# A two-level search for the first edges of quads, slot tables built group by group, degrees counted in a later pass

## The reference

```python
edge_index = jnp.stack([src, dst])
x = layernorm(x + L0(x, edge_index, edge_attr))
x = layernorm(x + L1(x, edge_index))
# L0: e = edge_attr @ W_edge + b_edge; msg = relu(x[src] + e)
#     agg = segment_sum(msg, dst); h = (1 + eps) * x + agg
#     h = relu(h @ W1 + b1) @ W2 + b2; batch norm over nodes, relu
# L1: deg = segment_sum(1, dst) + 1; dinv = rsqrt(deg)
#     layer(h, W, b): h = h @ W.T
#       agg = segment_sum(h[src] * dinv[src] * dinv[dst]) + own row; relu(agg + b)
#     three such layers
```

## Time and profile before

| | us |
|---|---|
| median of 3 runs | 4261.39 (4259.22 to 4263.67) |
| the profiled execution, its own time | 4236.74 |
| its span, first to last instruction | 4235.0 |
| PE, DVE, ACT, POOL busy, share of the span | 89%, 88%, 63%, 51% |
| constants | 0 to 21 |
| degrees | 21 to 196 |
| slot tables | 196 to 268 |
| GIN pass | 268 to 1475 |
| batch norm's scale | 1475 to 1488 |
| norm pass | 1488 to 2036 |
| three GCN passes | 2036 to the end |

### The profile page before, as it was taken

The page is one execution under the profiler, slowest core; times in us unless marked ns, Lnnn a source line. Parts: engine busy times, 40 slices in busy tenths (PEclk is TensorE's granted clock), DMA queues, the critical chain, the costliest instruction groups (busy, mean ns, idle before and its releaser), DMA issues. The chain is left out here.

```text
span 4235.0 us, 107970 instructions
## 1 busy us (share of the span) xinstructions
PE 3771.7 (89%) x27934; PEld 3481.4 (82%) x27934; DVE 3713.5 (88%) x10654; ACT 2649.3 (63%) x6276; POOL 2170.3 (51%) x1972
## 2 busy tenths in 40 slices
PE   6639999999999889999688889869889988999999
PEld 1139999999999768888688888868888887888887
DVE  8838898889889799999788888868888887999999
ACT  0016666666666578888677878757878885444444
POOL 0035444444444000000477777757777775777776
PEclk9869999999999989999899999989999999999999
DMA  0055555555555299999677767747767776999999
GB/s 24 1 98 166 162 159 158 158 158 159 160 159 159 70 324 375 374 374 376 217 211 214 214 211 218 213 151 213 217 208 215 219 216 197 315 311 309 312 311 287
DMA packets 871189, 909.87 MB, mean 215 GB/s; under 512 B 154170, under 2 KB 770580, under 8 KB 871060
## 3 DMA queue, kind: packets, MB, share of 16 engines
q1 hardware_dynamic: 744400, 702.74, 50.8%
q0 software_dynamic: 94080, 205.13, 17.9%
q10 hardware_dynamic: 32580, 0.52, 0.5%
HBM read 651.69 MB, written 308.28 MB: 227 GB/s over the span
## 5 line engine op out<-in xcount | busy, mean ns | idle before, releaser
L462 POOL DMA_INDIRECT rows<-ga_scratch,node_i x980 | 1081.4, 1103 | 997.5 <-POOLq L598 699.6
L462 POOL DMA_INDIRECT rows<-x_in,node_i x490 | 518.5, 1058 | 671.6 <-DVE raw L915 476.8
L462 POOL DMA_INDIRECT rows<-gb_scratch,node_i x490 | 567.1, 1157 | 182.3 <-issue 171.9
L490 PE MATMUL gcn_agg_ps<-gcn_rows_hi,gcn_select 128*128 128x256 f32 x2156 | 576.5, 302 | 33.9 <-DVE gcn_rows_lo L1260 33.9
L490 PE MATMUL gcn_agg_ps<-gcn_rows_lo,gcn_select 128*128 128x256 f32 x2156 | 542.8, 286 | 0.0
L1380 PE MATMUL fin_agg_ps<-rows,fin_select 128*128 128x256 f32 x2156 | 530.8, 380 | 0.0
L1279 ACT CAST gcn_rows_hi<-rows 128x768 fp32r<-128x768 f32 (+1 forms) x392 | 286.2, 731 | 331.9 <-DMA rows<-ga_scratch,node_i 162.3
L1380 PEld LDWEIGHTS fin_agg_ps<-rows,fin_select 128*128 128x128 f32 x2156 | 410.8, 191 | 56.2
L490 PEld LDWEIGHTS gcn_agg_ps<-gcn_rows_hi,gcn_select 128*128 128x128 f32 x2156 | 419.4, 195 | 34.8 <-DVE gcn_rows_lo L1260 34.8
L517 PE MATMUL gcn_g_ps<-g_hi,gcn_ht_hi 128*128 128x256 f32 x1568 | 441.7, 282 | 0.7 <-ACT gcn_g L1298 0.7
L862 ACT ACTIVATE h1t_hi<-h1t_ps,b_sb 128x256 fp32r<-128x256 f32 x392 | 164.8, 471 | 439.0 <-issue 346.2
(11 more groups left out here) (158 smaller groups left out, 12314.2 us busy)
## 6 DMA issues: line engine op xcount, KB each, us to landing
own<-x_in SPq DMA_DIRECT2D x196, 256.0 KB, 3.0
h_scratch<-h2t SPq DMA_DIRECT2D x196, 256.0 KB, 2.2
h2t_in<-h_scratch SPq DMA_DIRECT2D x196, 256.0 KB, 3.9
x_sb<-x_in SPq DMA_DIRECT2D x196, 256.0 KB, 4.9
x_scratch<-x SPq DMA_DIRECT2D x196, 256.0 KB, 5.0
ga_scratch<-g_out SPq DMA_DIRECT2D x196, 256.0 KB, 5.1
gcn_own<-ga_scratch SPq DMA_DIRECT2D x196, 256.0 KB, 2.9
gb_scratch<-gcn_g SPq DMA_DIRECT2D x196, 256.0 KB
```

Of the source, the lines that this page charges most:

```text
L462: pool.indirect_dma_start(out=c["rows"][:, slot, b], out_offset=None, in_=source[:, :], in_offset=bass.IndirectOffsetOnAxis(ap=c["node"][: ...
L490: last = nc.tensor.matmul(out[:, j], select[:, b, j * P:(j + 1) * P], rows[:, pair.odd + b], start=n == 0, stop=n == len(terms) - 1)
```

## The change

- `degrees` and `slot_tables` go; `search` takes their place. It loads only the destinations (a new input array `dst`), as 128 rows of 392. For each of the 98 quads, and each of the five tile limits 0, 128, ..., 512 from the quad's first node, a one-hot matrix chooses the row in which the limit lies, five float32 products on PE fetch these rows, and DVE counts the entries below the limit. First edges and the test for `fast` come from that.
- In the GIN pass the windows are loaded four quads at a time: SP loads group 0 ahead of the pass and group g + 2 at the beginning of group g, ACT loads group 1 ahead of its first step. DVE makes the tables of group g + 1 (seven operations on 20 columns) at the beginning of group g, ahead of the step's h0; at group 0 it makes those of group 0 as well. POOL waits for them once a group.
- The degrees are counted in the norm pass. DVE splits `place` into tile and node once; POOL writes five one-hot matrices of 128 columns for a quad; PE adds five products with 4 columns for a quad at the head of the even steps; DVE copies the counts, ACT takes the root and DVE does the Newton step for 16 tiles once a group.
- `general_sum` counts a histogram of its own in its first use, under `fast == 0`, and is skipped as before.

```diff
-def pipeline(eng, step):
+def pipeline(eng, step, begin=None):
     def group(number):
+        if begin is not None:
+            begin(number)
         for k in range(GROUP):
...
-def degrees(nc, keep, dram):
+def search(nc, keep, dram):
...
+                sp.dma_start(dst_i[:, 0:COLS], dram["dst"][0:P * COLS].rearrange("(p c) -> p c", p=P))
+                sp.dma_start(dst_i[:, COLS:COLS + 2],
+                             dram["dst"][COLS:COLS + P * COLS].rearrange("(p c) -> p c", p=P)[:, 0:2])
...
+                nc.vector.tensor_copy(rows[:, 0:COLS + 1], dst_i[:, 0:COLS + 1])
+                nc.vector.tensor_scalar(upto[:], limit[:], rows[:, COLS:COLS + 1], None, ALU.is_le)
+                nc.vector.scalar_tensor_tensor(out=chosen[:], in0=limit[:], scalar=rows[:, 0:1], in1=upto[:],
+                                               op0=ALU.is_gt, op1=ALU.mult)
+                nc.vector.tensor_tensor(falls[:], rows[:, 0:COLS], rows[:, 1:COLS + 1], ALU.is_gt)
+                nc.vector.tensor_reduce(broken[:, 6:7], falls[:], AX.X, ALU.add)
+                nc.vector.tensor_tensor(less[0:NQ], found[0:NQ, :, 0:COLS], own_limit..., ALU.is_lt)
+                nc.vector.tensor_reduce(count[0:NQ], less[0:NQ], AX.X, ALU.add)
+                nc.vector.tensor_tensor(partly[0:NQ], count[0:NQ], found[0:NQ, :, COLS + 2], ALU.mult)
+                nc.vector.tensor_tensor(before[0:NQ], partly[0:NQ], found[0:NQ, :, COLS + 1], ALU.add)
+                nc.vector.tensor_scalar(rel[0:NQ], before[0:NQ, 1:TILES + 1], before[0:NQ, 0:1], None, ALU.subtract)
...
+                for t in range(TILES + 1):
+                    nc.tensor.matmul(found[0:NQ, t, 0:COLS + 3], chosen[:, t:t + NT]..., rows[:])
+                nc.tensor.matmul(start_row[0:1, 0:NQ], before[0:NQ, 0:1], c["ident"][0:NQ, 0:NQ])
+                nc.tensor.matmul(broken_sum[:], c["ones"][:], nbroken[:])
...
# gather_quads
+        if tables is not None and quad % GROUP_QUADS == 0:
+            pool.wait_ge(tables, (quad // GROUP_QUADS + 1) * TABLE_STEPS)
...
# gin_pass, SP
+                def begin(number):
+                    if not isinstance(number, int) or number + 2 < TABLE_GROUPS:
+                        sp.wait_ge(windows_in, (number + 1) * LANDED)
+                        load_windows(sp, number + 2, windows_in)
+                load_windows(sp, 0, windows_in)
+                pipeline(sp, step, begin)
...
# gin_pass, ACT
+                load_windows(act, 1, windows_next)
...
# gin_pass, DVE
+                def begin(number):
+                    if isinstance(number, int) and number == 0:
+                        table(0)
+                    if not isinstance(number, int) or number + 1 < TABLE_GROUPS:
+                        table(number + 1)
...
# norm_pass, POOL
+                pool.wait_ge(split_done, 5)
+                for quad in range(NQ):
+                    if quad >= 2:
+                        pool.wait_ge(counted, quad - 1)
+                    for b in range(BLOCKS):
+                        last = nc.gpsimd.tensor_scalar(hot_node[:, quad % 2, b], c["iota16"][:, 0:P],
+                                                       node_in_tile[:, quad, b:b + 1], None, ALU.is_equal)
+                    last.then_inc(hot_done, 1)
...
# norm_pass, ACT
+                    if (pair := at(8)) and pair.place == 0:
+                        act.wait_ge(deg_steps, pair.group * DEG_STEPS + 1)
+                        nc.scalar.activation(root[:], deg[:], ACT.Sqrt).then_inc(rooted, 1)
...
# norm_pass, PE, first in the step
+                    if (pair := at(0)) and not pair.odd:
+                        pe.wait_ge(hot_done, pair.quad + 1)
...
+                        for b in range(BLOCKS):
+                            last = nc.tensor.matmul(deg_ps[:, first:first + 4], hot_node[:, pair.quad_slot % 2, b],
+                                                    hot_tile[:, bass.ds(pair.quad, 1), b]...)
+                        last.then_inc(counted, 1)
...
# norm_pass, DVE: seven operations on 490 and 1960 columns ahead of the steps (place to node_in_tile, hot_tile)
+                    if (pair := at(7)) and pair.place == 0:
+                        dve.wait_ge(counted, (pair.group + 1) * GROUP_QUADS if whole else NQ)
+                        nc.vector.tensor_tensor(deg[:], deg_ps[:, 0:GROUP_TILES], c["hist"]..., ALU.add)
+                    if (pair := at(9)) and pair.place == 0:
+                        degree(pair)   # reciprocal, mult, add, scale, reciprocal on 16 columns, each behind a wait
...
# gnn
-        degrees(nc, keep, dram)
-        slot_tables(nc, keep, dram)
+        search(nc, keep, dram)
```

More of the change, by code:

```diff
@@ L320, in _ @@
+                nc.vector.tensor_tensor(falls[:], rows[:, 0:COLS], rows[:, 1:COLS + 1], ALU.is_gt).then_inc(chain, 1)
                 dve.wait_ge(chain, 6)
[L321 to L329 removed]
@@ L453, in gather_quads @@
-def gather_quads(nc, pool, c, source, gathered, rows_free):
+                pe.wait_ge(chain, 5)
+                for t in range(TILES + 1):
+                    nc.tensor.matmul(found[0:NQ, t, 0:COLS + 3],
+                                     chosen[:, t:t + NT].rearrange("p (q t) -> p q t", t=TILES)[:, :, 0],
+                                     rows[:], start=True, stop=True).then_inc(looked, 1)
+                pe.wait_ge(chain, 11)
+                nc.tensor.matmul(start_row[0:1, 0:NQ], before[0:NQ, 0:1], c["ident"][0:NQ, 0:NQ],
+                                 start=True, stop=True).then_inc(looked, 1)
@@ L455, in gather_quads @@
+                pe.wait_ge(chain, 14)
+                nc.tensor.matmul(broken_sum[:], c["ones"][:], nbroken[:], start=True, stop=True).then_inc(looked, 1)
+def gather_quads(nc, pool, c, source, gathered, rows_free, tables=None):
     bound = pool.to_reg(NPAD - 1)
@@ L768, in gin_pass, with load_windows @@
          stats_done) = (m.sem("gin_" + n) for n in names.split())
+        LANDED = 16 * GROUP_QUADS
+        def load_windows(eng, number, landed):
+            for k in range(GROUP_QUADS):
+                q = number * GROUP_QUADS + k
+                start = eng.value_load(c["starts"][0:1, bass.ds(q, 1)], min_val=0, max_val=E)
+                eng.dma_start(c["window"][:, bass.ds(q, 1)].rearrange("p o b t -> p (o b) t"),
+                              dram["edges"][bass.ds(start, SLOTS), :].rearrange("(b p) t -> p b t", p=P))\
+                   .then_inc(landed, 16)
         with nc.Block() as block:
@@ L778, in step @@
                         s = pair.slot
-                        start = sp.value_load(c["starts"][0:1, bass.ds(pair.quad * 4, 1)], min_val=0, max_val=E)
+                        start = sp.value_load(c["starts"][0:1, bass.ds(pair.quad, 1)], min_val=0, max_val=E)
                         if pair.has(RING):
@@ L1067, in step @@
                         s = pair.slot
+                        if pair.place == 0:
+                            act.wait_ge(deg_steps, (pair.group + 1) * DEG_STEPS)
                         act.wait_ge(dense_done, pair.done())
@@ L1084, in _ @@
             def _(pe):
+                pe.wait_ge(split_done, 6)
                 def step(at):
+                    if (pair := at(0)) and not pair.odd:
+                        first = pair.quad_slot * 4
+                        pe.wait_ge(hot_done, pair.quad + 1)
+                        if pair.place == 0 and pair.has(GROUP):
+                            pe.wait_ge(deg_steps, pair.group * DEG_STEPS - (DEG_STEPS - 1))
+                        for b in range(BLOCKS):
+                            last = nc.tensor.matmul(deg_ps[:, first:first + 4], hot_node[:, pair.quad_slot % 2, b],
+                                                    hot_tile[:, bass.ds(pair.quad, 1), b].rearrange("p o t -> p (o t)"),
+                                                    start=b == 0, stop=b == BLOCKS - 1)
+                        last.then_inc(counted, 1)
                     if pair := at(3):
```

401 lines of the change are left out of this document (218 added, 183 removed).

## The result

| | before | after |
|---|---|---|
| median, us (4 runs each) | 4261.86 | 4092.86 |
| lowest and highest | 4259.22, 4263.67 | 4088.94, 4095.48 |
| profiled execution, own time (span) | 4236.74 (4235.0) | 4088.94 (4086.9) |

The ratio is 0.9605, with a 95% interval of 0.9589 to 0.962: 169 us less, where 126 were forecast. The time lies inside the range that was stated, 42 us under the forecast and 8 us above the lower end.

A forecast was written before the change was run, and what follows sets the result against it. Stages run one after another: DVE bounds the histogram and norm pass, PE the GIN pass. Front -219, GIN pass +23 and norm pass +70 sum to -126 us, so 4261.4 becomes 4135; range 4085 to 4185.

The forecast's parts named there:

- first rival: Norm pass: PE's five small products cost nothing, since PE has 10% and more of real room; 4103 us, chance 0.18.
- Front, -219: Ahead of the GIN pass: search replaces histogram and table loads, first attribute load at 51.8 against 271.09; bounds 212 and 226.
- Table on DVE, +23: GIN pass: table burst ahead of h0 makes PE stand still about 1.0 us, 23 times; ends nothing and 41 us.
- Degree chain, +31: Norm pass: DVE's copy of counts and five dependent operations take 1.25 us in each of 25 groups, all paid.
- Five products, +32: Norm pass: PE's products take 0.5 us, 0.44 of it paid 73 times; ends nothing and 69 us.
- POOL's matrices on the ports, +6: Norm pass: 490 one-hot matrices on POOL, 0.29 us each, sometimes hold DVE's `x1`; between 0 and 13 us.
- third rival: Norm pass: POOL's one-hot matrices hold DVE; in part 4175 us, chance 0.07; whole, 142 us, 4271, chance 0.02.
- the fourth: Norm pass: POOL becomes the bound, kernel slower than before; gain gone at 1.52 us a matrix, 4497 at 2.0; chance 0.03.
- Preamble, +1: Ahead of the norm pass's steps: DVE's split of `place` and POOL's first two quads, about 6 us against 4.9.
- Small operations at 0.28: DVE's tiny operations cost 0.28, not 0.20 us: tables 18 more, degrees 10 more, 4163 us; chance 0.14.
- Windows on SP at nothing: GIN pass: SP's four windows a group, 5.2 us, covered by loads' lead; up to 115 us if that were gone.
- the signs that the prediction named: Right: first attribute load 50 to 54, some 23 PE gaps, norm pass 600 to 625; wrong: `x1` over 0.40, PE awaiting POOL.

The follow-up runs named there:

- chip A: One of three chips of the follow-ups: kernel before 4671.6 us; changed kernel with products four times 4502.42, one one-hot matrix instead of five 4495.7, no Newton step 4481.59.

## Why the prediction was right in direction and 42 us short

- **The lower end of the range.** The prediction puts it at "the first rival with the front at its better bound, 4085", but that is 4103 - 7 = 4096. Only by this slip does the measured 4092.86 lie inside.
- **Front, -219.** Measured -220.0. The prices per column and per issue held (2.20 us for each wide operation, 2.2 from the last issue of a window to its landing). That the sum came out to 1 us has some luck in it: DVE had the destinations at 22.6 and not at 24.9, while the search took 13.7 us and not 12.7 (the five products 5.35 against 4.7), and from its end to the first attribute load it took 14.8 and not 14.2.
- **Table on DVE, +23.** Measured +15.6. The mechanism was right (h late, PE waits, paid once a group), both sizes were off. The burst was to take 1.2 us and takes 1.65: "5 x 0.20 and 2 x 0.09" left out three places where 0.3 us pass in front of an operation. The slack was to be 0.2 us and is 1.65 - 0.83 = 0.82. I read it from the earlier trace rows at 1421 us, in the drain of the pass, where PE's queue has other work ahead of that sum than in the middle. At the pairs where the tables fall, the kernel before has these rows (timeline, one pair in eight):

```profile
715.82 0.74 DVE L906 SCALAR_TENSOR_TENSOR h<-own,self_w,agg_ps 128x512 f32<-128x512 f32 x1
...
717.23 0.36 PE L490 MATMUL agg_ps<-msg_hi,gin_select 128*128 128x256 f32 x1
```

  From h's end to PE's start are 0.67 us there, not 0.35, and in the changed kernel a PE that waits for h starts 0.06 behind its listed end (699.30 to 699.36). That makes 0.6 of the 0.8 us; the other 0.2 were not traced.
- **Degree chain, +31.** What the norm pass has gained beyond POOL's share is 36.3 - 4.3 = 32.0 us. Four of the six operations are 25.8 of it by experiment; the other two are left with 6.2 by subtraction.
- **Five products, +32.** Measured nothing. This is the step that failed, twice: the products take 0.13 us and not 0.5, and "a slack of 0.06 at most" compared a z with the `res` of another pair, where z is ready 2.9 us ahead. The first rival (chance 0.18, 4103 us) was right on this term. Its argument, that PE is busy for 492 of 548 us and so has room, was the better one.
- **POOL's matrices on the ports, +6.** Measured 4.3, though half by luck: a matrix takes 0.63 us, not 0.29, so POOL is busy twice as long as I took, and a meeting costs a third of what I took (0.011 / 0.51 = 0.022 us against 6 / (392 x 0.23) = 0.067; the overlapping `x1` in the trace have 0.021). The third rival's argument that only `x1` and a few tiny operations stay clear of PSUM left out the statistics. The third rival and the fourth (POOL as the bound at 1.52 us a matrix) did not come.
- **Preamble, +1.** Measured +5.6. DVE's operations on 490 columns start 0.33 to 0.45 us apart, 2 us until POOL may begin; then the first matrix takes 2.6 us and the nine behind it 0.6 each, where I had taken 0.29 for each.
- **Small operations at 0.28** (second rival): they cost 0.25 in the degree chain and 1.65 / 7 = 0.24 in the table, so half-way to it.
- **Windows on SP at nothing:** right; with the table's place mended, the pass is as short as before with all windows in it.

Norm pass and turn together: 36.3 + 5.6 = 41.9 us measured, 70 forecast. All stages that the change touches sum to -220.0 + 15.6 + 41.9 = -162.5, which is 36.5 of the 43 us by which the forecast fell short; the timed difference is -169. The 6.5 us between are less than the spread of the last passes of the kernel before over two chips (2200.6 to 2232.5), and have no other cause that was shown. The choice to put the sum on the median, not on the profiled execution, was sound for that reason: that execution of before was 25 us quick, and its last passes are the shortest of all traces.

Of the signs that the prediction named, these came: the first attribute load at 51.1 us, 22 to 23 waits of PE for h, six small operations a group. These did not: DVE hardly waits for z (0.7 us in 4 waits, 1300 to 1750 us), the norm pass takes 590 us in the window of the earlier trace rows and not 600 to 625, and POOL's operations take 0.6 us and not 0.3. Two of its signs of being wrong came, `x1` over 0.40 us and a PE that waits for POOL at the start.

## What to carry to other kernels

Before a gap between two rows is called a slack, count both lists and see that the rows belong to the same pair; in a software pipeline the neighbour in time is often another iteration's. Read a slack in the steady middle of the pass and at the pair where the new work falls, not in fill or drain. Small serial work cost 0.25 us an operation here on the engine that bounds the stage, and nothing that shows in a standing wait or on an engine with idle time: eleven such operations a group, moved, gave 46 us (19.9 and 26.0). A range should be added up from its terms once more before it is written down.

## What the runs showed of the hardware that was not expected

- A weight load of a 128 x 128 bf16 matrix is listed with 0.10 us, yet five products with 4 columns pass in 0.13 us and twenty in 0.52: 0.026 us each. The listed durations overlap; here the distance between starts is the price.
- POOL's comparison of 128 float16 columns with a scalar from memory takes 0.60 us, or 0.67 where it meets `x1`, twice its selection of 128 float32 columns (0.292), and the first of them took 2.62; on 16 columns a POOL operation takes 0.20 to 0.22, like DVE's. The row of the tile in the changed kernel (shortest, median, longest in ns; 1280 to 1880 us):

```profile
L1074 POOL TENSOR_SCALAR hot_node<-iota,node_in_tile x490: 590/601/2621, 1285.5 to 1850.6; 128x128 bf16<-128x128 f16 x164
```

- The kernel before took 4248 to 4262 us in three of the four sets of runs and 4671.6 on chip A. Front, turn and norm pass agreed to 1.2 us there; the GIN pass was 114 us longer and the last passes 284 to 316. In the GIN pass (300 to 1400 us) ACT's waits had a line that the other trace of before lacks:

```profile
ACT h1t_hi L862 <- remote: 147.0, 32, 4.8
```

The passes that lengthened are those that gather rows; what held them was not tried. The granted clock explains little of the GIN pass (0.98 against 0.99 over the stage, with PE busy for 1210 of 1318 us); in the last passes it was 0.92 against 0.98, and PE was busy for 83% of them in place of 89%. Whether the lower clock there is a cause or follows from the waits is open. With PE already waiting there for other reasons, the table burst cost the changed kernels 6 to 8 us on A in place of 16.
